# Sending the stacked q/k pieces of an attention kernel in four-head groups, in 64 KB transfers, six under way

## The chip, the cores and the metric

The kernel runs on one core of a Trainium2 chip. The metric is the device time of one execution in microseconds, as the median of repeated runs. The program is launched once; everything from the loads of x and of the weights to the stores of the result is in the time.

## What is computed

The reference takes x of shape 4 x 1024 x 256 (four sequences) and applies two layers. Each layer normalises the rows, and adds an attention over 16 heads of 16 channels and a feed-forward part to x.

```
xn = layernorm(x)
x = x + attention0(xn) + ffn0(xn)     # layer 0: rotary positions, causal mask; ffn0 is a router over 32 slots, top 2
xn = layernorm(x)
x = x + attention1(xn) + ffn1(xn)     # layer 1: scores set to 0 (not to -inf) above the diagonal; ffn1 has sign weights
```

## The kernel before, in words

The work is cut into eight **stages**, k = 0 to 7. A stage is one sequence in one layer; the order is (sequence 0, layer 0), (1, 0), (0, 1), (1, 1), and then the same for sequences 2 and 3. The attention of a stage runs in four **groups** g of four heads.

Scores are wanted with float32 accuracy from bf16 matmuls. So q and k are each split into three bf16 pieces, and the products that matter are put under one another along the contracted dimension: QS and KS are stacks of six terms of 16 rows (96 rows), and three more rows of QS carry the negated row maxima, also in three pieces. The way of one stage:

- TensorE projects q and k in eight chunks c = 0 to 7 (`project`, L1012; VectorE finishes them in `projected`, L787). Chunks 0 to 3 hold the first eight heads (ot = 0), chunks 4 to 7 the other eight.
- ScalarE and GpSimd split each chunk in turn: `first_part` (L626, instruction at L633), `first_rest` (L569, L572), `second_part` (L635, L638), `third_part` (L575, L579). The pieces land in `parts`, which has room for eight heads, so `first_part` of chunk 4 has to wait until the first eight heads have been sent on, and that of chunk 0 of the next stage until the second eight have.
- SyncE sends the pieces into the stacks (`send_stack`, L492, the transfers at L500): twelve transfers of 256 KB for eight heads, all issued one behind the other, without a wait between them. A transfer reads 128 partitions of `parts` and writes 16 rows of a stack. Before the first, SyncE waits for the pieces, and for the scores of the stage before to have read the heads that are written over (L497).
- For each group, TensorE makes the scores once for their row maxima (`max_unit`, L1076, matmuls at L1083 and L1086; VectorE reduces them at L915), VectorE splits the maxima, TensorE turns them (L1092), VectorE copies them to nmT (L938), and ScalarE's queue sends nmT, 24 KB, into the three rows of QS (`send_maxima`, L654, the transfer at L658).
- Then TensorE makes the transposed scores with the maxima already taken off (`scores`, L1094, L1108 and L1111; the first one of a group waits for that transfer, L1098), ScalarE exponentiates (L673), and TensorE multiplies with the values (`weighted_values`, L1114, L1128).

The work of several stages overlaps: while stage k is in its scores, the projections, pieces and stacks of stage k + 1 are made. All engines take their steps **in an order that a planner on the host writes out beforehand** (`plan`, L83, and `run_plan`, L264). The planner gives each step a cost, a due time, a list of steps that it comes after, and a lag until others see its result; at each point it takes, for each engine, the step that can start first, and among equals the one due first. On the chip the order is fixed: a step that waits holds up all that stands behind it on its engine. The planner books a stack of eight heads with 27 us on SyncE and a lag of 3 us (L147), sent when the pieces are there and the stage before has finished the second of the two groups (L146); `first_part` of chunk 4 comes after it (L137). It books 3.5 us for the transfer of nmT (L205).

SyncE's order also holds the loads of x and the stores of the result (`load_x`, L486, `store`, L503). The load of x for stages 4 and 5 waits for the stores of stages 2 and 3.

Of the kernel before, what the change touches and what calls it, by code (L numbers as in the profile page):

```python
# [15 lines left out]
KC = D // P  # L16
# [14 lines left out]
BANK = 512  # L31
NW = 2 * 2 * KC
W_BANKS, ST_BANKS, PT_SLOTS = 3, 3, 2

# [46 lines left out]
def plan():  # L83
# [4 lines left out]
    def job(eng, step, cost, due, after, lag=60.0):  # L88
        jobs[eng, step] = (cost, due, after, lag)
# [16 lines left out]
    for k, (b, l) in enumerate(STAGES):  # L106
# [27 lines left out]
        for c in range(NW):  # L134
            kind, ot, hf = chunk(c)
            due = at(0.1 + 0.03 * c) if ot == 0 else at(0.5 + 0.05 * (c - 4))
            land = [("sp", ("stack", k, 0))] if ot else ([("sp", ("stack", k - 1, 1))] if k else [])  # L137
            job("pe", ("qk", k, c), mm(1024, 4), due, [("act", ("xT", k, 2 * hf + 1))], PE_LAG)
            job("dve", ("qk", k, c), dv(512) * (4 if l == 0 else 1), due,
                [("pe", ("qk", k, c))] + ([("pool", ("third", k, c - 2))] if c > 1 else [("pool", ("third", k - 1, NW - 2 + c))] if k else []))  # L140
            job("act", ("first", k, c), 640, due, [("dve", ("qk", k, c))] + land)
            job("pool", ("rest", k, c), 1180, due, [("act", ("first", k, c))])
            job("act", ("second", k, c), 640, due, [("pool", ("rest", k, c))])
            job("pool", ("third", k, c), 1180, due, [("act", ("second", k, c))])
        for ot in range(KC):
            gone = [("pe", ("st", k - 1, 2 * ot + 1, NEX - 1))] if k else []  # L146
            job("sp", ("stack", k, ot), 27000, at(0.2) if ot == 0 else at(0.7),  # L147
                [("pool", ("third", k, 4 * ot + 3))] + gone, 3000.0)
        xt = [("act", ("xT", k, i)) for i in range(4)]
        if l == 0:  # L150
            job("pe", ("router", k), 1700, at(0.22), xt, PE_LAG)
# [38 lines left out]
        for g in range(NG):  # L190
            gs = t0 + g * tg
            for i, (seg, qb, j, n, wd, diag) in enumerate(MAXU):
                due = gs - tg + 0.8 * tg * i / NMX
                job("pe", ("max", k, g, i), mm(n * wd, 1) + 60 * n * diag, due, [("sp", ("stack", k, g // 2))], PE_LAG)
                before = ("rows", k, g - 1) if g else (("rows", k - 1, NG - 1) if k else None)
                job("dve", ("max", k, g, i), dv(n * wd), due, [("pe", ("max", k, g, i))]
                    + ([("dve", ("split",) + before[1:])] if before else []))
            last = [("dve", ("max", k, g, i)) for i in range(NMX)]
            job("dve", ("split", k, g), 1100 + 400 * l, gs - 0.2 * tg, last + ([("dve", before)] if before else [])
                + ([("pool", ("ev", past[-1], g))] if l and past else []))  # L200
            job("pe", ("rows", k, g), 60, -1.0, [("dve", ("split", k, g))], PE_LAG)
            sent = [("act", ("send",) + before[1:])] if before else []
            job("dve", ("rows", k, g), 230, -1.0, [("pe", ("rows", k, g))] + sent)
            gone = [("pe", ("st", k - 1, g, NEX - 1))] if k else []
            job("act", ("send", k, g), 100, -1.0, [("dve", ("rows", k, g))] + gone, 3500.0)  # L205
            if l == 1:
                job("act", ("e", k, g), 200, gs - 0.1 * tg, [("dve", ("split", k, g))])
                used = [("dve", ("out", k, g - 1, t)) for t in range(2)] if g else (
                    [("dve", ("out", past[-1], NG - 1, t)) for t in range(2)] if past else [])
                job("pool", ("ev", k, g), 1150, gs, [("act", ("e", k, g))] + used  # L210
                    + [("dve", ("later", k, n)) for n in range(NT)])
            m = 2 * (k * NG + g)
            for u, (half, kb, j, n, w) in enumerate(EXPU):
                due = gs + tg * u / NEX
                ordinal = (k * NG + g) * NEX + u
                free = []
                if ordinal >= ST_BANKS:
                    o = ordinal - ST_BANKS
                    free = [("act", ("exp", o // NEX // NG, o // NEX % NG, o % NEX))]
                job("pe", ("st", k, g, u), mm(n * w, 1) + 60 * n * (kb >= 4 * half), due, [("act", ("send", k, g))] + free, PE_LAG)  # L220
                v = PVS.index((half, kb))
                free = []
                if u == PV_FIRST[v]:
                    o = (k * NG + g) * NPV + v - PT_SLOTS
                    free = [("pe", ("pv", o // NPV // NG, o // NPV % NG, o % NPV))] if o >= 0 else []
                job("act", ("exp", k, g, u), ac(n * w), due, [("pe", ("st", k, g, u))] + free)
            for v, (half, kb) in enumerate(PVS):
                due = gs + tg * PV_LAST[v] / NEX - 500
                cols = BANK - max(kb - 4 * half, 0) * P
                free = []  # L230
                if kb == 0 and m + half >= 2:
                    o = m + half - 2
                    free = [("act", ("ocopy", o // 2 // NG, o // 2 % NG, o % 2))]
                job("pe", ("pv", k, g, v), mm(cols, 4) + 60, due, [("act", ("exp", k, g, PV_LAST[v]))] + free
                    + ([("dve", ("v", k, i)) for i in range(4)] if g == 0 and v == 0 else []), PE_LAG)
            for t in range(2):
                due = gs + tg * PV_LAST[HALF_END[t]] / NEX
                o = m + t - 2
                free = [("pe", ("out", o // 2 // NG, o // 2 % NG, o % 2))] if o >= 0 else []
                job("act", ("ocopy", k, g, t), ac(512), due - 600, [("pe", ("pv", k, g, HALF_END[t]))] + free)  # L240
                job("pe", ("out", k, g, t), 460, due, [("act", ("ocopy", k, g, t))], PE_LAG)
                gone = [("pe", ("aT", k - 1, 2 * t + i)) for i in range(2)] if k and g == 0 else []
                job("dve", ("out", k, g, t), 1250 + 1000 * l, due, [("pe", ("out", k, g, t))] + gone
                    + ([("pool", ("ev", k, g))] if l else []))
# [98 lines left out]
def build(nc, a, out):  # L343
    ctx = ExitStack()
    with ctx:
# [86 lines left out]
        normed = Signal(sem("normed"), NT)  # L432
        biased = Signal(sem("biased"))
        part1, rest1, part2, part3 = (Signal(sem(n), NW) for n in ("part1", "rest1", "part2", "part3"))
        stacked = [Signal(sem(f"stacked{o}"), 12, step=16) for o in range(KC)]
        moe_logits = Signal(sem("moe_logits"))
        moe_exp = Signal(sem("moe_exp"))
        suffix_ok = Signal(sem("suffix_ok"), 6)
# [39 lines left out]
        def _(sp):  # L478
# [10 lines left out]
                    sp.wait_ge(*y_out[k % 2].upto(stores_before(k), 0))  # L489
                sp.dma_start(x[:, k % 2, :, :], a["x"][b:b + 1].rearrange("o (n p) d -> p (o n) d", p=P)).then_inc(x_in[k % 2].sem, 16)  # L490

            def send_stack(k, ot):  # L492
                sp.wait_ge(*part3.upto(k, NW // 2 * (ot + 1)))
                sp.wait_ge(*part2.upto(k, NW // 2 * (ot + 1)))
                sp.wait_ge(*part1.upto(k, NW // 2 * (ot + 1)))
                if k:
                    sp.wait_ge(*st_full.upto(k - 1, (2 * ot + 2) * NEX))  # L497
                for term in range(len(Q_PARTS)):
                    for stack, kind, which in ((QS, 0, Q_PARTS), (KS, 1, K_PARTS)):
                        sp.dma_start(stack[term * DH:(term + 1) * DH, ot * HC * T:(ot + 1) * HC * T],  # L500
                                     parts[:, which[term], kind, :]).then_inc(stacked[ot].sem, 16)

            def store(k, h):  # L503
                sp.wait_ge(*empty(("wo", k, 2 * h + 1)))
# [106 lines left out]
        def _(act):  # L611
# [14 lines left out]
            def first_part(k, c):  # L626
                kind, ot, hf = chunk(c)
                act.wait_ge(*empty(("qk", k, c)))
                if c == 4:
                    act.wait_ge(*stacked[0].upto(k, 12))  # L630
                if c == 0 and k:
                    act.wait_ge(*stacked[1].upto(k - 1, 12))
                act.activation(parts[:, 0, kind, hf * BANK:(hf + 1) * BANK], proj[:, c % 2, :], ACT.Copy).then_inc(part1.sem, 1)  # L633

            def second_part(k, c):  # L635
# [338 lines left out]
        def _(pe):  # L974
# [101 lines left out]
            def max_unit(k, g, i):  # L1076
                seg, qb, j, n, wd, diag = MAXU[i]
                bank = bank_for(("max", k, g, i))
                if i == 0:
                    pe.wait_ge(*stacked[g // 2].upto(k, 12))  # L1080
                for q in range(n):
                    h = (g * GH + j + q) * T
                    mm = pe.matmul(bank[:, q * wd:(q + 1) * wd], QS[0:KR, h + qb * P:h + (qb + 1) * P],  # L1083
# [78 lines left out]
def tables():  # L1162
    half = DH // 2
    inv = (np.float32(1.0) / np.power(np.float32(10000.0), np.arange(half, dtype=np.float32) / np.float32(half))).astype(np.float32)
    freqs = np.arange(T, dtype=np.float32)[None, :] * inv[:, None]
    cos = np.repeat(np.cos(freqs), HC, axis=0).astype(np.float32)
    sin = np.repeat(np.sin(freqs), HC, axis=0).astype(np.float32)
    return np.concatenate([cos, cos]), np.concatenate([sin, -sin])


# [37 lines left out]
```

## Time and profile before

| | us |
|---|---|
| median of 3 runs | 1730.38 |
| lowest, highest | 1730.19, 1731.06 |
| the profiled execution, its own time | 1736.93 |
| its span, from the first to the last instruction | 1735.2 |
| TensorE matmul busy (share of the span) | 1551.3 (89%) |
| VectorE busy | 1204.3 (69%) |
| ScalarE busy | 803.8 (46%) |
| GpSimd busy | 238.6 (14%) |
| mean granted TensorE clock, as a share of 2.4 GHz | 0.947 |

The terms below are held against the profiled execution, which was 6.55 us longer than the median. Busy shares are averages over stages that differ; what stops TensorE in a stretch is read from the waits and from the chain of work that ended last.

### The profile page before, as it was taken

To read this page: it belongs to the slowest core of one execution; us is meant where nothing else is said; L and a number is where in the kernel's file an instruction comes from. 1 tells how busy PE (TensorE), PEld (TensorE's weight loads), DVE (VectorE), ACT (ScalarE), POOL (GpSimd) and SP (SyncE) were. 2 spreads that over 40 slices of the span, in tenths; PEclk is the share of its full clock that TensorE was granted. 3 is DMA by queue.
4 is the path that set the end of the run, shared out by engine and by line. 5 is a ranking of instruction groups with operands and counts; after the bars stand their busy time and mean duration, and the time that the engine had idled before them with its cause. 6 is when DMAs were issued, how large, how long until landed. Compare 5 with 4: busy or idle time off the path is not lost.

```text
span 1735.2 us, 26902 instructions
## 1 busy us (share of the span) xinstructions
PE 1551.3 (89%) x10398; PEld 807.8 (47%) x10398; DVE 1204.3 (69%) x2674; ACT 803.8 (46%) x1548; POOL 238.6 (14%) x196
## 2 busy tenths in 40 slices
PE   2787995999999999997959989899999998999998
PEld 1444443464445544463424644445444564446444
DVE  7864873767776777778747678676677677776871
ACT  1112443446555555634434456244555554553655
POOL 5221201102021211112011002010211121021000
PEclk9888897999999989998989999899999999999998
DMA  4336033042063206070230341502406150607000
GB/s 165 39 35 74 2 37 38 1 52 24 10 66 45 31 2 74 11 113 1 33 42 1 45 79 15 60 1 30 45 2 74 19 57 2 74 2 98 2 2 25
DMA packets 44095, 66.28 MB, mean 38 GB/s; under 512 B 7328, under 2 KB 18880, under 8 KB 43968
## 3 DMA queue, kind: packets, MB, share of 16 engines
q1 hardware_dynamic: 40800, 63.77, 28.9%
q8 instruction: 83, 1.36, 0.4%
q10 hardware_dynamic: 3168, 0.79, 0.3%
q14 instruction: 44, 0.36, 0.1%
HBM read 9.23 MB, written 4.19 MB: 8 GB/s over the span
## 4 chain that ended last, share of the span: by engine, by line
PE 75%; DVE 13%; DMA 6%; ACT 3%; issue 2%; SPq 1%; POOL 0%; DVEq 0%; ACTq 0%; POOLq 0%
PE WB L984 22%; PE O L1128 16%; PE WB L1083 14%; PE ST L1108 14%; DMA QS<-nmT 5%; PE ST L1111 3%; PE WB L1086 3%; DVE mxa L915 3%; ACT PT L673 2%; DVE rope_b L805 2%; PE WB L1136 1%; DVE mxb L915 1%; PE WB L1009 1%; PE WB L1050 1%; DVE WB L808 1%
## 5 line engine op out<-in xcount | busy, mean ns | idle before, releaser
L673 ACT ACTIVATE PT<-ST 128x512 f32<-128x512 f32 (+1 forms) x1216 | 626.1, 577 | 595.3 <-PE ST L1111 460.1
L915 DVE TENSOR_REDUCE mxa<-WB 128x1 f32<-128x512 f32 (+3 forms) x864 | 537.5, 664 | 161.6 <-PE WB L1086 94.5
L1108 PE MATMUL ST<-QS,KS 99*128 99x512 bf16 (+3 forms) x1536 | 436.3, 337 | 68.0 <-DMA QS<-nmT 53.4
L1083 PE MATMUL WB<-KS,QS 96*128 96x512 bf16 (+3 forms) x1536 | 454.8, 339 | 17.3 <-DVE proj L809 5.6
L1128 PE MATMUL O<-PT,Vaug 128*17 128x512 f32 (+3 forms) x3072 | 323.6, 497 | 5.6 <-ACT PT L673 3.3
L1108 PEld LDWEIGHTS ST<-QS,KS 99*128 99x128 bf16 x1536 | 149.6, 100 | 256.3 <-ACT PT L673 102.2
L1083 PEld LDWEIGHTS WB<-KS,QS 96*128 96x128 bf16 x1536 | 148.9, 100 | 251.4 <-DVE mxa L915 77.6
L915 DVE TENSOR_REDUCE mxb<-WB 128x1 f32<-128x384 f32 (+3 forms) x352 | 210.3, 635 | 24.1 <-PE WB L1086 22.4
L1086 PE MATMUL WB<-negmask,identb 128*128 128x128 bf16 x1024 | 204.4, 226 | 0.0
L1111 PE MATMUL ST<-negmaskT,identb 128*128 128x128 bf16 x1024 | 201.3, 225 | 0.0
L572 POOL TENSOR_TENSOR proj<-proj,parts 128x512 f32<-128x512 f32 x64 | 73.9, 1160 | 597.8 <-ACT parts L633 597.6
L1086 PEld LDWEIGHTS WB<-negmask,identb 128*128 128x128 bf16 x1024 | 103.7, 101 | 28.4 <-issue 14.3
L1111 PEld LDWEIGHTS ST<-negmaskT,identb 128*128 128x128 bf16 x1024 | 103.3, 101 | 13.6 <-issue 2.1
L1128 PEld LDWEIGHTS O<-PT,Vaug 128*17 128x17 f32 x3072 | 52.7, 96 | 111.1 <-ACT PT L673 66.9
L567 POOL TENSOR_TENSOR x<-x,brow 128x2048 f32<-128x2048 f32 x8 | 36.3, 4539 | 373.3 <-DVE xn L784 373.3
L633 ACT ACTIVATE parts<-proj 128x512 bf16<-128x512 f32 x64 | 39.5, 629 | 90.2 <-DVE proj L809 52.4
L579 POOL TENSOR_TENSOR parts<-proj,parts 128x512 bf16<-128x512 f32 x64 | 73.8, 1159 | 41.2 <-ACT parts L638 41.2
L984 PE MATMUL WB<-xT,w_k 128*128 128x512 f32 x128 | 65.8, 638 | 9.5 <-DVE attn L956 4.3
L805 DVE SCALAR_TENSOR_TENSOR rope_b<-WB,bcol,sin 64x512 f32<-64x512 f32 x64 | 48.0, 750 | 37.3 <-PE WB L984 36.1
L984 PE MATMUL WB<-xT,w_q 128*128 128x512 f32 x128 | 67.8, 655 | 1.5 <-DVE proj L809 1.2
L984 PE MATMUL WB<-w_u,xT 128*128 128x512 f32 x128 | 64.8, 631 | 2.2 <-DVE Vaug L898 1.9
L651 ACT ACTIVATE ghT<-WB 128x512 f32<-128x512 f32 x32 | 19.1, 597 | 93.3 <-PE WB L1050 92.1
(140 smaller groups left out, 1402.9 us busy)
## 6 DMA issues: line engine op xcount, KB each, us to landing
QS<-parts SPq DMA_DIRECT2D x96, 256.0 KB, 13.7
KS<-parts SPq DMA_DIRECT2D x96, 256.0 KB, 15.2
x<-in_x SPq DMA_DIRECT2D x4, 1024.0 KB, 5.5
out<-x SPq DMA_DIRECT2D x8, 512.0 KB, 13.5
QS<-nmT ACTq DMA_DIRECT2D x32, 24.0 KB
w_q<-in_w_q SPq DMA_DIRECT2D x2, 256.0 KB, 6.2
w_k<-in_w_k SPq DMA_DIRECT2D x2, 256.0 KB, 6.1
cos<-in_cos SPq DMA_DIRECT2D x1, 512.0 KB, 5.4
```

What stands on the lines that cost most here:

```text
L572: pool.tensor_tensor(proj[:, c % 2, :], proj[:, c % 2, :], parts[:, 0, kind, hf * BANK:(hf + 1) * BANK], ALU.subtract).then_inc(rest1.sem, 1)
L579: pool.tensor_tensor(parts[:, 2, kind, tok], proj[:, c % 2, :], parts[:, 1, kind, tok], ALU.subtract).then_inc(part3.sem, 1)
L633: act.activation(parts[:, 0, kind, hf * BANK:(hf + 1) * BANK], proj[:, c % 2, :], ACT.Copy).then_inc(part1.sem, 1)
L673: act.activation(PT[:, q % PT_SLOTS, j:j + n, 0:wd], src, ACT.Exp, scale=float(SCALE[STAGES[k][1]])).then_inc(exp_done.sem, 1)
L805: ins = dve.scalar_tensor_tensor(rope_b[to:to + P // 2, :], bank[half, :], bcol[half, kind, ot:ot + 1], sin[half, tok], ALU.add, ALU.mult)
L915: dve.tensor_reduce(dst, bank, AX.X, ALU.max).then_inc(emptied, 1)
L984: mm = pe.matmul(dst, lhsT, rhs, start=(i == 0), stop=(i == len(pairs) - 1))
L1083: mm = pe.matmul(bank[:, q * wd:(q + 1) * wd], QS[0:KR, h + qb * P:h + (qb + 1) * P], KS[0:KR, h + seg * BANK:h + seg * BANK + wd], start= ...
L1086: mm = pe.matmul(bank[:, (q + 1) * wd - P:(q + 1) * wd], identb[:, :], negmask[:, :], start=False, stop=True)
L1108: mm = pe.matmul(ST[:, o + i * wd:o + (i + 1) * wd], KS[0:KM, h + kb * P:h + (kb + 1) * P], QS[0:KM, h + q0:h + q0 + wd], start=True, stop ...
L1111: mm = pe.matmul(ST[:, o + i * wd:o + i * wd + P], identb[:, :], negmaskT[:, :], start=False, stop=True)
L1128: mm = pe.matmul(O[32 * j:32 * j + VA, (half + 1) * BANK - cols:(half + 1) * BANK], Vaug[:, kb, h * VA:(h + 1) * VA], PT[:, slot, j, 0:col ...
```

## The change

A stack is sent for four heads at a time, in 24 transfers of 64 KB. A transfer reads 32 partitions of `parts` and writes 8 rows of a stack (even or odd channels, `par`). There are six semaphores, the lanes; transfer n takes lane n mod 6 and is issued only when the transfer before it on that lane has landed. Whoever waited for a stack now waits for all six lanes. For this the columns of Wq and Wk (and the rotary tables) are laid out on the host so that the four heads of a group lie on 32 neighbouring partitions. The planner's stack step is now for four heads, with 13.5 us on SyncE and a lag of 2.5 us, after the stage before has finished that one group; the planned cost of a step of `weighted_values` rises from 60 to 230 ns above its columns.

```diff
+LANES = 6
-            land = [("sp", ("stack", k, 0))] if ot else ([("sp", ("stack", k - 1, 1))] if k else [])
+            land = [("sp", ("stack", k, g)) for g in (0, 1)] if ot else ([("sp", ("stack", k - 1, g)) for g in (2, 3)] if k else [])
...
-        for ot in range(KC):
-            gone = [("pe", ("st", k - 1, 2 * ot + 1, NEX - 1))] if k else []
-            job("sp", ("stack", k, ot), 27000, at(0.2) if ot == 0 else at(0.7),
-                [("pool", ("third", k, 4 * ot + 3))] + gone, 3000.0)
+        for g in range(NG):
+            gone = [("pe", ("st", k - 1, g, NEX - 1))] if k else []
+            job("sp", ("stack", k, g), 13500, at(0.2 + 0.1 * g) if g < 2 else at(0.5 + 0.1 * g),
+                [("pool", ("third", k, 4 * (g // 2) + 3))] + gone, 2500.0)
...
-                job("pe", ("max", k, g, i), mm(n * wd, 1) + 60 * n * diag, due, [("sp", ("stack", k, g // 2))], PE_LAG)
+                job("pe", ("max", k, g, i), mm(n * wd, 1) + 60 * n * diag, due, [("sp", ("stack", k, g))], PE_LAG)
...
-                job("pe", ("pv", k, g, v), mm(cols, 4) + 60, due, [("act", ("exp", k, g, PV_LAST[v]))] + free
+                job("pe", ("pv", k, g, v), mm(cols, 4) + 230, due, [("act", ("exp", k, g, PV_LAST[v]))] + free
...
-        stacked = [Signal(sem(f"stacked{o}"), 12, step=16) for o in range(KC)]
+        lane = [Signal(sem(f"stack_lane{i}"), 16, step=16) for i in range(LANES)]
...
-            def send_stack(k, ot):
+            def send_stack(k, g):
+                ot, hh = g // 2, g % 2 * 32
...
                 if k:
-                    sp.wait_ge(*st_full.upto(k - 1, (2 * ot + 2) * NEX))
+                    sp.wait_ge(*st_full.upto(k - 1, (g + 1) * NEX))
+                n = 0
                 for term in range(len(Q_PARTS)):
                     for stack, kind, which in ((QS, 0, Q_PARTS), (KS, 1, K_PARTS)):
-                        sp.dma_start(stack[term * DH:(term + 1) * DH, ot * HC * T:(ot + 1) * HC * T],
-                                     parts[:, which[term], kind, :]).then_inc(stacked[ot].sem, 16)
+                        for par in range(2):
+                            turn = lane[n % LANES]
+                            if k or g or n >= LANES:
+                                sp.wait_ge(*turn.upto(k, 4 * g + n // LANES))
+                            src = parts[par * 64 + hh:par * 64 + hh + 32, which[term], kind, :]
+                            row = term * DH + par * (DH // 2)
+                            sp.dma_start(stack[row:row + DH // 2, g * GH * T:(g + 1) * GH * T], src).then_inc(turn.sem, 16)
+                            n += 1
...
                 if c == 4:
-                    act.wait_ge(*stacked[0].upto(k, 12))
+                    for turn in lane:
+                        act.wait_ge(*turn.upto(k, 8))
                 if c == 0 and k:
-                    act.wait_ge(*stacked[1].upto(k - 1, 12))
+                    for turn in lane:
+                        act.wait_ge(*turn.upto(k, 0))
...
                 if i == 0:
-                    pe.wait_ge(*stacked[g // 2].upto(k, 12))
+                    for turn in lane:
+                        pe.wait_ge(*turn.upto(k, 4 * g + 4))
...
-    cos = np.repeat(np.cos(freqs), HC, axis=0).astype(np.float32)
+    cos = np.tile(np.repeat(np.cos(freqs), GH, axis=0), (2, 1)).astype(np.float32)
...
-    cols = np.arange(D).reshape(KC, HC, DH // 2, 2).transpose(0, 3, 2, 1).ravel()
+    cols = np.arange(D).reshape(KC, 2, GH, DH // 2, 2).transpose(0, 4, 1, 3, 2).ravel()
```

## Rows read from the trace of the kernel before

**Rows 1.** The page's chain of work that ended last: shares by engine, by line

```profile
PE 75%; DVE 13%; DMA 6%; ACT 3%; issue 2%; SPq 1%; POOL 0%; DVEq 0%; ACTq 0%; POOLq 0%
```

**Rows 2.** Waits of TensorE: engine, line, releaser: us in total, times, longest

```profile
PE ST L1108 <- DMA QS<-nmT: 53.4, 8, 18.1
```

**Rows 3.** TensorE's timeline where it stood longest: start, us, instruction, idle before

```profile
159.56 0.61 PE L1108 MATMUL ST<-QS,KS 99*128 99x512 bf16 x1 [9.57 <-DMA QS<-nmT]
...
277.24 0.61 PE L1108 MATMUL ST<-QS,KS 99*128 99x512 bf16 x1 [18.07 <-DMA QS<-nmT]
...
886.15 0.61 PE L1108 MATMUL ST<-QS,KS 99*128 99x512 bf16 x1 [16.32 <-DMA QS<-nmT]
...
1109.47 0.61 PE L1108 MATMUL ST<-QS,KS 99*128 99x512 bf16 x1 [5.49 <-DMA QS<-nmT]
```

**Rows 4.** The chain in order of time: transfers of nmT on it, start, us

```profile
211.15 2.67 DMA QS<-nmT
...
255.16 22.03 DMA QS<-nmT
```

**Rows 5.** Issues of stack transfers, all (L500), and two ends of one stack on SyncE

```profile
L500 SPq DMA_DIRECT2D QS<-parts x96: 547/610/994, 71.7 to 1574.0; - x96
...
246.41 0.55 SPq L500 DMA_DIRECT2D QS<-parts  x1
...
253.53 0.62 SPq L500 DMA_DIRECT2D KS<-parts  x1
```

**Rows 6.** Stretches: busy us (instructions) of PE, PEld, DVE, ACT, POOL; PEclk, DMA share, GB/s

```profile
1.90:14.00 12.10, 0.63 (x2) 0.50 (x2) 5.69 (x2) 1.65 (x3) 11.64 (x8) 1.00 1.01 338
...
74.50:101.00 26.50, 23.12 (x81) 13.94 (x81) 15.16 (x29) 2.99 (x5) 0.00 (x0) 0.88 1.03 108
...
255.00:277.00 22.00, 4.17 (x18) 1.92 (x15) 4.97 (x9) 0.00 (x0) 0.00 (x0) 0.65 0.96 101
277.00:370.00 93.00, 91.39 (x605) 46.31 (x606) 63.83 (x124) 47.56 (x92) 9.17 (x8) 0.97 0.01 1
```

**Rows 7.** DMA queue of ScalarE (packets, MB, share), and the issues on it

```profile
q10 hardware_dynamic: 3168, 0.79, 0.3%
...
QS<-nmT ACTq DMA_DIRECT2D x32, 24.0 KB
```

**Rows 8.** ScalarE's timeline: the first piece of chunk 4, in stages 0, 1, 2 and 7

```profile
101.80 1.15 ACT L633 ACTIVATE parts<-proj 128x512 bf16<-128x512 f32 x2 [2.51 <-DMA KS<-parts]
...
296.12 1.19 ACT L633 ACTIVATE parts<-proj 128x512 bf16<-128x512 f32 x2
...
504.60 1.14 ACT L633 ACTIVATE parts<-proj 128x512 bf16<-128x512 f32 x2
...
1518.82 1.15 ACT L633 ACTIVATE parts<-proj 128x512 bf16<-128x512 f32 x2 [0.52 <-DMA KS<-parts]
```

**Rows 9.** SyncE's timeline: first transfers of the stacks of stage 0 and stage 2

```profile
71.66 0.67 SPq L500 DMA_DIRECT2D QS<-parts  x1
...
72.37 0.59 SPq L500 DMA_DIRECT2D KS<-parts  x1
...
473.97 0.55 SPq L500 DMA_DIRECT2D QS<-parts  x1
```

**Rows 10.** Stage 2's last third piece of chunks 0 to 3, and the next nmT

```profile
434.18 1.15 POOL L579 TENSOR_TENSOR parts<-proj,parts 128x512 bf16<-128x512 f32 x1 [0.74 <-ACT parts L638]
...
436.10 0.76 ACTq L658 DMA_DIRECT2D QS<-nmT  x1
```

**Rows 11.** SyncE around the store of stage 2, and VectorE's first use of the load

```profile
741.11 0.60 SPq L500 DMA_DIRECT2D KS<-parts  x1
749.32 5.33 SPq L506 DMA_DIRECT2D out<-x  x2
767.29 0.38 SPq L490 DMA_DIRECT2D x<-in_x  x1
...
777.93 2.70 DVE L746 BATCH_NORM_STATS2 stats<-x 128x6 f32<-128x256 f32 x8
```

More of the change, by code:

```diff
@@ L1165, in tables @@
     freqs = np.arange(T, dtype=np.float32)[None, :] * inv[:, None]
-    cos = np.repeat(np.cos(freqs), HC, axis=0).astype(np.float32)
-    sin = np.repeat(np.sin(freqs), HC, axis=0).astype(np.float32)
+    cos = np.tile(np.repeat(np.cos(freqs), GH, axis=0), (2, 1)).astype(np.float32)
+    sin = np.tile(np.repeat(np.sin(freqs), GH, axis=0), (2, 1)).astype(np.float32)
     return np.concatenate([cos, cos]), np.concatenate([sin, -sin])
```

## The prediction

> **What bounds the kernel now.** I read the shares of the chain first: 75% of it is TensorE, 6% a DMA [rows 1]. TensorE is the bound, so what counts is what makes it stand idle. Its waits, ordered by what ended them, have one DMA at their head: the first score matmul of a group waited for the transfer of nmT, 53.4 us in 8 waits, the longest 18.1 [rows 2]. Four of them, 9.57, 18.07, 16.32 and 5.49 us, are 49.5 us of that [rows 3]. The reader should see that this is no property of the transfer. On a quiet chip nmT takes 2.67 us from its issue to the first matmul; issued at 255.16, just after a stack whose twelve transfers went out from 246.41 to 254.15, it takes 22.03 us, the time in which that stack drains [rows 4, 5]. In that stretch TensorE is busy 4.17 of 22 us at a granted clock of 0.65, against 0.97 in the stretch behind it [rows 6]; 1.0 is 2.4 GHz, so part of it ran at the 1.2 GHz level after the wait. A small transfer stands behind 3 MB. The change is aimed there: never more than 6 x 64 KB ahead of it.
>
> So much speaks for it. Against it stands a second reading, of the rate. While the inputs load, the 16 DMA engines are full (share 1.01) and move 338 GB/s; while a stack is sent they are just as full (1.03) and move 108 GB/s [rows 6]. The loads write all 128 partitions, the stack 16 rows at a time. The engines are held up by something that depends on the shape, and the change halves the rows again, to 8.
>
> **What a group of 24 transfers takes.** The trace has no transfer to 8 rows, so I bound it. Lower end: SyncE's pace, 24 x 0.61 us [rows 5] + 2.7 us until the last is seen [rows 4] = 17.3 us; the 6 lanes never bind then. Upper end: the rate follows the rows, 54 GB/s, so 1.57 MB take 29.1 us, and with 2 us for the last, 31 us. I take 29 us, near the upper end, because the nearest row is the stack transfer itself: engines full, and rate far below the loads'. The planner books 13.5 + 2.5 = 16 us, so in my case the plan is 13 us short for each group; at the lower end only 1.3.
>
> Of how many engines such a transfer uses, the queue of nmT tells something: 3168 packets in 32 transfers are 99 each, 96 source rows and 3 more, and nmT is written to 3 rows [rows 7]. The Trainium skill (DMA: Bandwidth & Descriptors, "Why a DMA increments its semaphore by 16 and not by 1") says that a transfer runs on the largest number of engines, up to 16, that divides the outermost sizes of both its sides, each adding one to the semaphore: 3 for nmT, which the 3 extra packets agree with, and 8 for the new transfers. The skill (SBUF — State Buffer, "Door 1: The DMA port swizzle") gives 16 neighbouring partitions four ports and about 109 GB/s, which the 108 agrees with, and 8 would reach two; an estimate from that page is 54 GB/s or 29 us a group, a rule against this change, where SyncE's pace alone would give 17.3.
>
> **Part by part**, against the profiled execution (1736.9 us, span 1735.2; the median is 6.5 lower).
>
> 1. Stage 0. The first piece of chunk 4 waits for the first eight heads. They were sent from 71.66 [rows 9] and ScalarE went on at 101.80 after 2.51 us idle [rows 8]. Two groups at 29 us, the second's issue beginning 2 us before the first has landed, end at 71.7 + 56 = 128: 26 us late. Behind that wait on ScalarE stand the copies of the hidden part, and TensorE's banks behind them. VectorE has maxima to reduce meanwhile, so I take 15. Ends: 2 (pace 17.3) and 26.
>
> 2. Stages 1 to 7, same wait. The planner puts ScalarE's step right after the stack's booked landing, now 16 instead of 30 us after the stage before has finished its second group. In the trace the stack of stage 2 is sent at 473.97 and ScalarE's step starts at 504.60, 30 us later; stages 3, 6 and 7 do the same, the last at 1518.82 with a DMA as its releaser [rows 8, 9]. With 29 us the step stands some 13 us too early in a fixed order; the exponentials of the running stage are queued behind it, and TensorE has only three score banks. I take 8 us for each of these four, 32. In stages 1, 4 and 5 ScalarE came to it long after the landing: in stage 1 the stack was issued from 246.41 [rows 5], landed some 30 us later, and the step ran at 296.12 [rows 8], 20 us on. That covers most: 2 each, 6. Sum 38. Ends: 0 and 7 x 13 = 91.
>
> 3. The waits for nmT. At most six transfers ahead: 6 x 29/24 = 7.3 us instead of up to 22. The four long waits shrink to some 4 us of idling each, and the long ones give back their lower clock: -32. But stacks are now sent four times a stage, each starting when a group's scores end, which is about when the next nmT is sent. In stage 1 the pieces of the next stage are ready at 435.33 and nmT leaves at 436.10 [rows 10]; before, nothing was in flight there. I count ten such sends. A wait of 4 us is covered by other matmuls now; with some 7 to 9 us, 3 us each stay: +30. Net -2. Ends: -49 (all four long waits gone, nothing new) and +30.
>
> 4. SyncE itself. It is held by a group for as long as the group takes, where twelve issues took 7.7 us [rows 5]. The last issue before the store of stage 2 was at 741.11, the store left at 749.32, x was loaded at 767.29, and VectorE used it at 777.93 [rows 11]. That stack began 7.1 us before its last issue [rows 5], at 734; with SyncE held for 26 us from there the store moves by some 10 us, and VectorE waits in order for the load. Twice (stages 4 and 5), 4 us each after what VectorE has in hand: +8. Ends: 0 and 20.
>
> 5. Six waits instead of one before a group's maxima on TensorE, 32 x 5 more. The trace has no row for a wait that is already met; between nothing and the 0.04 us that SyncE's program takes from the end of one issue to the next [rows 9], 0 to 6 us: +3. ScalarE's extra waits, twice a stage, are hidden by its idle half (46% busy).
>
> 6. The planner's other order. 170 ns more for each weighted-value step shifts what is put beside what on every engine. Which way, no row tells: 0, with ends of 15 us either way.
>
> Layout and tables are made on the host: nothing on the chip.
>
> Sum: 15 + 38 - 2 + 8 + 3 = +62 us: 1799 for a profiled execution, **1792 us** for the median. This case's own range is 1745 to 1848: down by half of steps 1 and 2 (27) and 20 for the order and the idling; up by 9 in step 1, 32 in step 2 (some 16 us in each of the four stages) and 15 in step 6.
>
> **The rivals.**
>
> A. Transfers flow at SyncE's pace and it is faster. That needs six transfers under way to overlap in the memory where two neighbouring ones didn't before: the new ones alternate between the lower and upper 8 rows of a term, so at any time more than 8 rows are being written. Then a group takes 17.3 us, an nmT has at most 6 x 0.61 = 3.7 us ahead, the long waits give back 45 us, ten new ones cost 1.5 us each, steps 1 and 2 cost 2 + 7, SyncE frees early enough, step 5 costs 3: -18, and some 5 us come back as clock [rows 6]: 1707, with 1685 to 1735 around it. For it: the engines are full without moving much, so they have room. Against it: the twelve transfers of a stack change to other rows after every second one, and drain at 108 GB/s all the same [rows 6]. It decides at about 20 us a group.
>
> B. The rate lies between, a group takes 20 to 22 us, and what the nmT waits give back is paid again at the first pieces (about 7 us of the total for each us of a group): no change, 1730.
>
> C. The worse end of my case, as one mechanism: the wait at chunk 4 is not softened at all, because ScalarE feeds both the score banks and the projections, and every stage pays the full 13 us (91) and stage 0 26: 1730 + 91 + 26 - 2 + 8 + 3 = 1856. It decides where TensorE finds nothing else to do behind a held ScalarE.
>
> That the change doesn't do what it says is no rival here: the queue ahead of nmT is shorter in any case.
>
> **How the numbers follow.** My case has 0.55, C 0.05, A 0.32, B 0.08. Both signs hold much, so the range must reach into A: 1692 to 1848 leaves out the lower part of A (about 0.1) and the tail above. A difference of 0.2% (3.5 us) is about what measurement of this kernel can tell from none. Faster: A's 0.32 with a little of B, 0.33. Same: most of B, 0.07. Slower: 0.60.
>
> **What would show it.** Right: the share of the DMA engines and the rate in a group's stretch (about 54 GB/s, the last landing near 29 us after the first issue); ScalarE idle before the first piece of chunk 4 with a DMA as its releaser, in stage 0 by 15 us or more and in stages 2, 3, 6, 7 by some 8 to 13; no wait for nmT above 10 us, but more of them. Wrong: a group that lands in under 20 us, so that ScalarE's wait stays at 1 to 3 us and TensorE's total on nmT falls below 20; then A holds. If groups are slow and the total is not, ScalarE's wait was covered and step 2 is the mistake.

## The result, and the profile after

The changed kernel takes 1752.78 us (median, 1751.65 to 1756.17), the kernel before 1730.29 us beside it: 22.5 us slower, a ratio of 1.0133 (95% interval 1.0115 to 1.015). The profiled execution took 1751.65 us, with a span of 1749.9.

First the page's chain of work that ended last, shares of the span by engine and then by line. Lines have moved: the stack transfers are L511, the first piece L646, the exponentials L686, the scores L1122, the weighted values L1142.

```profile
PE 70%; DMA 12%; DVE 9%; SPq 3%; ACT 3%; issue 2%; POOL 0%; ACTq 0%; DVEq 0%; POOLq 0%
PE WB L997 20%; PE O L1142 15%; PE ST L1122 13%; PE WB L1097 13%; DMA KS<-parts 5%; DMA QS<-parts 4%; PE ST L1125 3%; SPq L511 3%; DMA QS<-nmT 2%; PE WB L1100 2%; ACT PT L686 2%; DVE mxa L928 2%; DVE rope_b L818 2%; PE WB L1150 1%; PE WB L1022 1%
```

Before, DMAs had 6% of it [rows 1], 5% for nmT, and the stacks were not among the lines that the page lists. Now nmT has 2%, and the stacks themselves (5% and 4%), with SyncE's issues between them (3%), have come in with 12%. The change did what it aimed at, and something else took the place. The waits say what; these are TensorE's (us in total, times, longest):

```profile
PE ST L1122 <- ACT PT L686: 35.2, 26, 9.2
PE ST L1122 <- DMA QS<-nmT: 22.5, 13, 3.6
PE O L1142 <- ACT PT L686: 21.7, 11, 8.3
...
PE WB L997 <- ACT ghT L664: 8.5, 1, 8.5
...
PE WB L1097 <- DMA KS<-parts: 7.6, 1, 7.6
```

The wait for nmT, 53.4 us before [rows 2], is 22.5, and its longest 3.6 instead of 18.1. But TensorE now stands 56.9 us behind ScalarE's exponentials, in pieces of up to 9 us. In the kernel before the same two waits were 15.3 us:

```profile
PE ST L1108 <- ACT PT L673: 12.0, 25, 2.2
...
PE O L1128 <- ACT PT L673: 3.3, 8, 1.0
```

What held ScalarE in the changed kernel stands in its own waits:

```profile
ACT parts L646 <- DMA KS<-parts: 69.9, 8, 14.0
```

Eight waits, one for each stage: the first piece of chunk 4, which may not overwrite `parts` until both groups of the first eight heads have landed. In ScalarE's timeline (start, us, instruction, idle before), stages 0 and 7, to be held against [rows 8], with stage 7's next instruction:

```profile
116.23 1.15 ACT L646 ACTIVATE parts<-proj 128x512 bf16<-128x512 f32 x2 [12.33 <-DMA KS<-parts]
...
1526.86 1.15 ACT L646 ACTIVATE parts<-proj 128x512 bf16<-128x512 f32 x2 [13.97 <-DMA KS<-parts]
1527.91 1.06 ACT L686 ACTIVATE PT<-ST 128x512 f32<-128x512 f32 x2
```

The idle times were 2.51 and 0.52 us. The next instruction behind the held one is an exponential that was long ready, and TensorE comes back with it, after 8.31 us (TensorE's timeline):

```profile
1528.54 0.63 PE L1142 MATMUL O<-PT,Vaug 128*17 128x128 f32 x8 [8.31 <-ACT PT L686]
```

The transfers: SyncE's timeline, the first and the last pair of issues of a quick group (stage 2, g = 0) and of a slow one (stage 7, g = 1), and the first pair of stage 0:

```profile
426.13 1.39 SPq L511 DMA_DIRECT2D QS<-parts  x2
...
442.06 1.39 SPq L511 DMA_DIRECT2D KS<-parts  x2
...
1502.59 1.39 SPq L511 DMA_DIRECT2D QS<-parts  x2
...
1520.71 1.60 SPq L511 DMA_DIRECT2D KS<-parts  x2
...
69.95 1.56 SPq L511 DMA_DIRECT2D QS<-parts  x2
```

In stage 0 two groups, issued from 69.95, let ScalarE go on at 116.23: 46.3 us, or about 23 for each. The slow group of stage 7 went from 1502.59 to ScalarE's start at 1526.86: 24.3 us. The quick one issues a pair every 1.43 us and is never held, which puts it at 17.3 us for the issues and some 2 for the last landing. The planner books 16. The rates in the slow group and then in the quick one (busy us of PE, PEld, DVE, ACT, POOL, then PEclk, DMA share, GB/s):

```profile
1503.00:1526.00 23.00, 17.14 (x123) 8.96 (x123) 12.91 (x29) 5.64 (x12) 1.11 (x1) 0.94 0.50 70
...
426.00:445.00 19.00, 17.84 (x118) 8.56 (x118) 12.57 (x30) 9.31 (x18) 0.10 (x1) 0.82 0.38 85
```

In these two stretches the 16 engines are busy 0.50 and 0.38 of the time, where a stack of before filled them all (1.03) [rows 6].

### The profile page after: what moved, and what is told of

It reads as the page before. It is cut to its first block, busy times and chain, and to the rows that moved or that the text cites. A ratio compares the mean times of both kernels' runs of the same rounds, so it can differ in the third digit from the quotient of the medians.

```text
span 1749.9 us, 27604 instructions
## 1 busy us (share of the span) xinstructions
PE 1558.8 (89%) x10398; PEld 803.3 (46%) x10398; DVE 1191.9 (68%) x2674; ACT 801.0 (46%) x1548; POOL 238.8 (14%) x196
## 4 chain that ended last, share of the span: by engine, by line
PE 70%; DMA 12%; DVE 9%; SPq 3%; ACT 3%; issue 2%; POOL 0%; ACTq 0%; DVEq 0%; POOLq 0%
PE WB L997 20%; PE O L1142 15%; PE ST L1122 13%; PE WB L1097 13%; DMA KS<-parts 5%; DMA QS<-parts 4%; PE ST L1125 3%; SPq L511 3%; DMA QS<-nmT 2%; PE WB L1100 2%; ACT PT L686 2%; DVE mxa L928 2%; DVE rope_b L818 2%; PE WB L1150 1%; PE WB L1022 1%
## 5 line engine op out<-in xcount | busy, mean ns | idle before, releaser
L686 ACT ACTIVATE PT<-ST 128x512 f32<-128x512 f32 (+1 forms) x1216 | 626.7, 578 | 551.9 <-PE ST L1125 397.3
L1122 PE MATMUL ST<-QS,KS 99*128 99x512 bf16 (+3 forms) x1536 | 436.7, 338 | 60.0 <-ACT PT L686 35.2
L1097 PE MATMUL WB<-KS,QS 96*128 96x512 bf16 (+3 forms) x1536 | 457.7, 342 | 25.5 <-DVE proj L822 10.8
L1142 PE MATMUL O<-PT,Vaug 128*17 128x512 f32 (+3 forms) x3072 | 327.6, 501 | 23.9 <-ACT PT L686 21.7
L1122 PEld LDWEIGHTS ST<-QS,KS 99*128 99x128 bf16 x1536 | 149.1, 100 | 254.3 <-ACT PT L686 129.8
L646 ACT ACTIVATE parts<-proj 128x512 bf16<-128x512 f32 x64 | 39.7, 627 | 159.5 <-DMA KS<-parts 69.9
L1142 PEld LDWEIGHTS O<-PT,Vaug 128*17 128x17 f32 x3072 | 51.7, 95 | 132.4 <-ACT PT L686 84.9
L818 DVE SCALAR_TENSOR_TENSOR rope_b<-WB,bcol,sin 64x512 f32<-64x512 f32 x64 | 48.0, 750 | 54.5 <-PE WB L997 53.4
L997 PE MATMUL WB<-w_v,ghT 128*128 128x256 f32 x256 | 65.3, 400 | 8.6 <-ACT ghT L664 8.5
```

What stands on the lines that cost most here:

```text
L686: act.activation(PT[:, q % PT_SLOTS, j:j + n, 0:wd], src, ACT.Exp, scale=float(SCALE[STAGES[k][1]])).then_inc(exp_done.sem, 1)
L818: ins = dve.scalar_tensor_tensor(rope_b[to:to + P // 2, :], bank[half, :], bcol[half, kind, ot:ot + 1], sin[half, tok], ALU.add, ALU.mult)
L997: mm = pe.matmul(dst, lhsT, rhs, start=(i == 0), stop=(i == len(pairs) - 1))
L1122: mm = pe.matmul(ST[:, o + i * wd:o + (i + 1) * wd], KS[0:KM, h + kb * P:h + (kb + 1) * P], QS[0:KM, h + q0:h + q0 + wd], start=True, stop ...
L1142: mm = pe.matmul(O[32 * j:32 * j + VA, (half + 1) * BANK - cols:(half + 1) * BANK], Vaug[:, kb, h * VA:(h + 1) * VA], PT[:, slot, j, 0:col ...
```

## The experiments

The theory: the shorter queue ahead of nmT is a gain; the loss is the planner's, which books a group of four heads with 16 us where it takes 19 to 24, and so puts steps that need a stack too early in orders that can't bend. Rivals: the smaller transfers are too slow whatever the plan says; or the loss comes with the other planner cost (the weighted-value step, 60 to 230 ns).

**e1_truthful_plan.** The changed kernel, one booking altered.

```diff
-            job("sp", ("stack", k, g), 13500, at(0.2 + 0.1 * g) if g < 2 else at(0.5 + 0.1 * g),
-                [("pool", ("third", k, 4 * (g // 2) + 3))] + gone, 2500.0)
+            job("sp", ("stack", k, g), 18500, at(0.2 + 0.1 * g) if g < 2 else at(0.5 + 0.1 * g),
+                [("pool", ("third", k, 4 * (g // 2) + 3))] + gone, 4500.0)
```

> The changed kernel with one planner cost altered: a group's stack is booked with 18.5 us on SyncE and a lag of 4.5 us (23 us in all) in place of 13.5 and 2.5. In the changed kernel's trace a group takes 19 to 23 us to its last packet, and ScalarE stands 69.9 us in 8 waits before the first piece of chunk 4. Theory (the loss is the plan's: steps that need a stack are put 7 us too early in a fixed order): ScalarE's wait falls below 20 us, TensorE's idle time behind ScalarE (56.9 us at the scores and the weighted values) by 30 to 45 us, the time to 1705 to 1725 us, below the kernel before. Rival (the slower transfers themselves cost the time, whatever the plan says): ScalarE's wait stays above 50 us or turns into other waits, the time stays at 1745 to 1760 us.

Measured: 1689.85 us, a ratio to the kernel before of 0.9755 (0.9728 to 0.9781); 63 us less than the changed kernel, with the same transfers. Its waits:

```profile
PE ST L1122 <- DMA QS<-nmT: 17.4, 13, 2.8
PE ST L1122 <- ACT PT L686: 16.0, 25, 2.8
...
ACT parts L646 <- DMA KS<-parts: 10.8, 5, 4.7
```

ScalarE's wait went from 69.9 to 10.8 us, TensorE's behind ScalarE at the scores from 35.2 to 16.0. The rival that the transfers as such cost the time falls: they are the same as in the changed kernel, and the kernel is 42 us faster than the kernel before the change. That gain is not the short queue's alone, as this kernel also keeps the raised cost of the weighted-value step (e3 below). It came out 15 us below the expected 1705 to 1725.

**e9_late_chunk4.** Where in the plan the 63 us lie. The changed kernel with its booking kept, and only ScalarE's step planned at the true time, by an empty step that stands for the landing.

```diff
-            land = [("sp", ("stack", k, g)) for g in (0, 1)] if ot else ([("sp", ("stack", k - 1, g)) for g in (2, 3)] if k else [])
+            land = [("sp", ("landed", k))] if ot else ([("sp", ("stack", k - 1, g)) for g in (2, 3)] if k else [])
...
+        job("sp", ("landed", k), 0, at(0.3), [("sp", ("stack", k, g)) for g in (0, 1)], 7000.0 if k else 12000.0)
...
-            run = {"load": load_x, "stack": send_stack, "store": store}
+            run = {"load": load_x, "stack": send_stack, "store": store, "landed": lambda k: None}
```

> The changed kernel (1752.8 us) with the planner told the truth at one place alone: ScalarE's first piece of chunk 4 is planned 7 us (in stage 0: 12 us) after the booked landing of the second group; SyncE's booking of 13.5 + 2.5 us stays for all else that needs a stack (the first maxima, chunk 0 of the next stage, the stores). Booking the whole truthfully gave 63 us back (1689.9). Theory (nearly all of the loss is ScalarE's wait at chunk 4, with the exponentials behind it): ScalarE's wait for a stack falls from 69.9 to 20 us or less, and 45 us or more come back: 1685 to 1708 us. Rival (the loss is spread over all that needs a stack): 1715 to 1745 us.

Measured: 1701.89 us, ratio 0.9806 (0.9777 to 0.9835). Of the 63 us, 51 come back at this one step; ScalarE's waits:

```profile
ACT parts L647 <- DMA KS<-parts: 8.3, 5, 3.3
```

So most of the loss of the change comes from where the plan puts the first piece of chunk 4. The other 12 us go with what else needs a stack. Two of TensorE's waits hint at where, though no run gives either a price of its own:

```profile
PE ST L1123 <- DMA QS<-nmT: 22.1, 13, 2.9
...
PE WB L1098 <- DMA KS<-parts: 7.9, 1, 7.9
```

The wait for the first stack of stage 0 is as long as in the changed kernel (7.6) and does not appear among the waits of e1; the wait for nmT is 22.1 us, where e1 has 17.4.

**e2_after_pv60 and e3_before_pv230.** The other planner cost, taken back on the changed kernel and put alone on the kernel before.

```diff
-                job("pe", ("pv", k, g, v), mm(cols, 4) + 230, due, [("act", ("exp", k, g, PV_LAST[v]))] + free
+                job("pe", ("pv", k, g, v), mm(cols, 4) + 60, due, [("act", ("exp", k, g, PV_LAST[v]))] + free
```

> The changed kernel with the planned cost of a weighted-value step put back from 230 to 60 ns above its columns; the transfers stay as changed. Theory (the stacks' booking makes the loss, this cost only shuffles the order): within 12 us of the changed kernel's 1753 us, ScalarE's wait for the stack still 40 us or more. Rival (the new order that this cost makes is what loses): 1730 us or less.

Measured: 1759.33 us, ratio to before 1.0146 (1.0119 to 1.0173), 6.5 us above the changed kernel by the medians, with ScalarE's wait at 51.4 us. The two intervals of the ratio overlap (the changed kernel's is 1.0115 to 1.015), so the 6.5 us are not clear of noise. The rival falls: without this cost the change is no better.

```diff
-                job("pe", ("pv", k, g, v), mm(cols, 4) + 60, due, [("act", ("exp", k, g, PV_LAST[v]))] + free
+                job("pe", ("pv", k, g, v), mm(cols, 4) + 230, due, [("act", ("exp", k, g, PV_LAST[v]))] + free
```

> The kernel before with only that planned cost raised from 60 to 230 ns; transfers and stacks as before. Theory (it only shuffles the order): within 12 us of 1730 us, the long waits for nmT still there (40 us or more of TensorE's idle time). Rival (this cost is the loss of the change): 1745 us or more.

Measured: 1714.82 us, ratio 0.9894 (0.9873 to 0.9914). The long waits for nmT are still there (49.3 us in 9 waits), and it is 17 us faster all the same. So my own expectation (within 12 us) was off as well: on the kernel before, this cost alone is a gain. On the changed kernel no gain is shown.

**e4_before_two_lanes.** The gain without the small transfers: the kernel before, its 256 KB transfers to 16 rows, and two of them under way.

```diff
+LANES = 2
-        stacked = [Signal(sem(f"stacked{o}"), 12, step=16) for o in range(KC)]
+        lane = [Signal(sem(f"stack_lane{i}"), 24 // LANES, step=16) for i in range(LANES)]
...
+                n = 0
...
+                        turn = lane[n % LANES]
+                        if k or ot or n >= LANES:
+                            sp.wait_ge(*turn.upto(k, 12 // LANES * ot + n // LANES))
                         sp.dma_start(stack[term * DH:(term + 1) * DH, ot * HC * T:(ot + 1) * HC * T],
-                                     parts[:, which[term], kind, :]).then_inc(stacked[ot].sem, 16)
+                                     parts[:, which[term], kind, :]).then_inc(turn.sem, 16)
+                        n += 1
```

(The waits in `first_part` and `max_unit` go over both lanes in the same way.)

> The kernel before, with its twelve transfers of 256 KB to 16 rows, but only two under way: two semaphores, each transfer waits for the one two before it; layout and planner costs as before. This is the change's gain without its smaller transfers. Theory (the gain comes from the short queue ahead of nmT, the loss from the slow groups): a stack still drains in about 30 us, nmT finds at most two transfers (4.6 us) ahead, TensorE's idle time on it falls from 53 to 15 us or less, ScalarE's wait for a stack stays below 15 us, the time is 1690 to 1710 us. Rival (a shorter queue is worth nothing, what TensorE doesn't wait for here it waits for elsewhere): 1725 us or more.

Measured: 1683.68 us, ratio 0.9711 (0.9681 to 0.9741): 48 us gained, with the planner untouched, and somewhat more than the 1690 to 1710 us allowed. TensorE's wait for nmT, and the stretch in which the kernel before stood for 18.07 us [rows 3], stage 0's third nmT:

```profile
PE ST L1117 <- DMA QS<-nmT: 5.4, 6, 2.3
```

```profile
246.00:277.00 31.00, 29.70 (x188) 15.19 (x187) 21.93 (x46) 13.94 (x27) 4.50 (x4) 1.00 0.46 79
```

From 53.4 to 5.4 us, and 48 us of time: nearly all of what TensorE stood behind nmT was time lost. ScalarE's wait for a stack is 9.0 us: the stacks still take what the plan books. In the stretch the granted clock is 1.00; in the wait of before it was 0.65 [rows 6].

**e8_three_lanes.** The same with `LANES = 3`.

```diff
-LANES = 2
+LANES = 3
```

> The kernel before with three transfers of 256 KB under way in place of two (1683.7 us). Theory (each transfer ahead costs nmT 2.3 us, two already fill the engines): stacks still 30 us, TensorE's idle time on nmT up from 5 us to 8 to 15, the time 1683 to 1696 us. Rival (two under way left the engines idle at times, and the stack lands sooner with three): the time below 1680 us.

Measured: 1700.27 us, ratio 0.9809 (0.979 to 0.9829); TensorE's wait for nmT is 17.7 us in 8 waits, the longest 4.5. One transfer of 256 KB more ahead of nmT cost 17 us of the time, somewhat over the 13 that the theory allowed; 12 of them stand in TensorE's wait for nmT. The rival falls.

**e5_two_lanes_short_booking.** The fault by itself: e4 with the stack's booking 7 us too short, on transfers that suit the plan otherwise.

```diff
-            job("sp", ("stack", k, ot), 27000, at(0.2) if ot == 0 else at(0.7),
+            job("sp", ("stack", k, ot), 20000, at(0.2) if ot == 0 else at(0.7),
```

> The kernel before with two transfers of 256 KB under way (1683.7 us), and now with the stack's planned cost on SyncE put from 27 to 20 us: the transfers are the same and still take 30 us, but the plan believes 23. This is the change's fault by itself, 7 us of misbooking, on transfers that are not slow for their plan otherwise. Theory (a booking 7 us short costs what the changed kernel lost against its truthful plan, 63 us, scaled by half as many stacks): ScalarE's wait for a stack rises from 9 to 40 us or more, the time to 1710 to 1750 us. Rival (the planner's order is only shuffled by it): within 10 us of 1684 us.

Measured: 1746.71 us, ratio to before 1.0078 (1.0048 to 1.0107), and 63 us above e4. The waits are those of the changed kernel over again:

```profile
PE ST L1117 <- ACT PT L681: 36.3, 28, 8.3
PE O L1137 <- ACT PT L681: 24.6, 11, 8.3
...
PE ST L1117 <- DMA QS<-nmT: 7.7, 7, 2.1
```

with ScalarE's wait for the stack at 58.9 us in 7. A number in a host-side plan, 7 us wrong, costs 63 us on transfers that did not change. The time lies in the range of the theory, but its scaling did not hold: half as many stacks cost as much. That the two losses are the same 63 us is not explained.

**e6_twelve_lanes.** What sets a group's 19 to 24 us: e1 with twelve lanes.

```diff
-LANES = 6
+LANES = 12
```

(with two transfers a group on each lane instead of four in the counts of the waits)

> The changed kernel with the truthful plan (1689.9 us), now with twelve lanes in place of six. It asks what sets the 19 to 23 us of a group. If six lanes bind (a transfer lands too late for the next on its lane): SyncE no longer waits for lanes, every group takes 18.5 to 19.5 us, and nmT finds up to twelve transfers ahead, so TensorE's idle time on it rises from 17 to 20 to 35 us; time within 10 us of 1690 us. If writing 8 rows at a time is the limit (about 71 GB/s where lanes bound): the slow groups still take 22 to 23 us, issues only come earlier, nmT waits longer all the same, time 1690 to 1710 us.

Measured: 1697.09 us, ratio 0.9789 (0.9764 to 0.9814). SyncE no longer waits for lanes (2.1 us in 9 waits, 39.8 in 142 with six). A group's issues now take 17.1 us; a slow group and a quick one in the same columns as above:

```profile
671.30:694.00 22.70, 22.45 (x186) 9.97 (x185) 19.08 (x46) 14.93 (x30) 1.11 (x1) 1.00 0.50 71
406.90:425.40 18.50, 17.61 (x110) 7.36 (x111) 11.11 (x24) 8.57 (x17) 0.00 (x0) 0.72 0.38 87
```

The slow group was issued by 688.4 and its DMA share stays at 0.50 and 71 GB/s to the end of the stretch. So it isn't the six lanes that make a group slow: with twelve a slow one drains no faster. In others the same transfers keep up with SyncE. TensorE's wait for nmT was 18.7 us, hardly more than with six lanes; the first reading expected 20 to 35, and the second a longer wait too, so neither had this right.

**e7_two_lanes_pv230.** The two gains together: e4 with the weighted-value cost of e3.

```diff
-                job("pe", ("pv", k, g, v), mm(cols, 4) + 60, due, [("act", ("exp", k, g, PV_LAST[v]))] + free
+                job("pe", ("pv", k, g, v), mm(cols, 4) + 230, due, [("act", ("exp", k, g, PV_LAST[v]))] + free
```

> The kernel before with two transfers under way, and the planned cost of a weighted-value step raised from 60 to 230 ns, as the change has it. On the kernel before this cost alone gave 17 us, on the changed kernel 6.5. Theory (it gives TensorE's order a truer price, and adds to the shorter queue): 1660 to 1678 us. Rival (both take away the same idle time, or it only shuffles): 1680 us or more.

Measured: 1671.41 us, ratio 0.9643 (0.9622 to 0.9664). They nearly add (48 and 17 alone): 61 us below the kernel before beside it, 81 below the changed kernel. With two transfers under way the planner cost gains 12 us. It is the fastest version of the study, without smaller transfers and without a new layout.

## Why the prediction was right or wrong

It was right that the kernel gets slower, and why: the mechanism, with ScalarE held before chunk 4 and TensorE behind it, is the one that the trace and e9 show. It was wrong in size, +62 against +22.5 us. Of its own signs, some came: no wait for nmT above 10 us but more of them (13, the longest 3.6), and ScalarE held in stages 2, 3, 6 and 7, for 6.34, 11.76, 9.24 and 13.97 us (some 8 to 13 forecast). Others did not: no group moved at 54 GB/s or took 29 us, and ScalarE's wait in stage 0 was 12.33 us and not 15 or more. Rival A's sign ("TensorE's total on nmT falls below 20") did not come, though narrowly, with 22.5. Rival B had the length of a group about right (20 to 22 us) and the balance wrong: it forecast no change. By the steps:

- *The length of a group*, taken as 29 us. Measured 19 to 24. Neither end was right. The lower end of 17.3 us had 14.6 for the issues; a quick group's issues alone took 17.3. And the rate did not follow the rows down to 54 GB/s, as the slow group moved 70. By the rule of the Trainium skill that the prediction cites (DMA: Bandwidth & Descriptors, "Why a DMA increments its semaphore by 16 and not by 1"), 8 of 16 engines were to be in use, and the slow group's share of 0.50 agrees with it. The estimate of 54 GB/s that the prediction worked out from two ports of the Trainium skill (SBUF — State Buffer, "Door 1: The DMA port swizzle") is not what was measured, and the measurement decides. Why some groups drain at 85 to 87 GB/s with a share of 0.38 and others at 70 with 0.50 was not tried.
- *Step 1*, +15. TensorE stood 7.6 us for the first stack and 8.5 behind ScalarE: 16.1. The first of the two I had not seen. (The forecast's range counts 9 us above the 15, where the step's own end of 26 leaves 11.)
- *Step 2*, +38. TensorE's idle time behind ScalarE at the scores and weighted values rose from 15.3 to 56.9 us: 41.6. That the term fits is in part luck, as errors offset one another. The plan was short by some 7 us for a group and not by 13. But less of that was softened: in stages 2, 3, 6 and 7 TensorE stood 6.3, 6.1, 9.2 and 8.3 us behind ScalarE's 6.3, 11.8, 9.2 and 14.0, where I let it stand 8 of 13. And stages 1, 4 and 5 were not covered: ScalarE was idle there for 5.4, 5.6 and 5.2 us, and TensorE behind it for 3.5, 4.0 and 4.2, where I allowed 2. By e1, being true to the transfers is worth 63 us in all, where steps 1 and 2 have 53.
- *Step 3*, -2. **This is the step that failed**, the term that was mis-sized. I let the four long waits keep 4 us each and gave ten new ones 3 us, so that about 51 of the 53 us stayed. (By its own figures the four fall from 49.5 to 16 us, -33.5 and not -32, before any clock is given back.) They fell to 22.5, a gain of 31. The long ones kept 1.5 to 2.1 us each, 7 in all; the other nine waits have 15 together, where the kernel before had 4 in four, so the new idling is 11 us and not 30. The size came from the group's length: 6 x 29/24 = 7.3 us ahead of nmT, and "some 7 to 9 us" for a transfer. In the changed kernel's chain of work that ended last, the longest nmT is this one (start, us):

```profile
825.68 5.53 DMA QS<-nmT
```

  Stage 0, g = 2, is the case of the 18.07 us [rows 3]. TensorE's timeline there, and the stretch up to it in the columns of [rows 6]:

```profile
262.62 0.39 PE L1122 MATMUL ST<-QS,KS 99*128 99x512 bf16 x1 [1.96 <-DMA QS<-nmT]
```

```profile
255.00:262.50 7.50, 5.56 (x26) 2.91 (x24) 6.02 (x16) 0.00 (x0) 0.00 (x0) 1.00 0.56 74
```

  TensorE's granted clock is 1.00 there, against 0.65 in the wait of before. And e4 shows the worth of such a wait, 48 us of time for 48 us of wait.
- *Step 4*, +8. The load of x moved the other way; what that is worth in time was not measured. SyncE's timeline after stage 2's last group:

```profile
750.40 1.39 SPq L511 DMA_DIRECT2D KS<-parts  x2
751.83 1.52 SPq L517 DMA_DIRECT2D out<-x  x2
756.55 0.38 SPq L492 DMA_DIRECT2D x<-in_x  x1
```

  The store left 2.5 us later than before, but x was loaded at 756.55 instead of 767.29 [rows 11]: the load waits for the store, so the store landed in under 5 us. In the kernel before the load left 18 us after the store's first issue, about when the stack ahead of it had drained (some 30 us from 734). That the store was late there because of that stack is argued from these times. What I had seen of nmT I should have seen of the store.
- *Step 5*, +3, was not measured alone. e6 doubles those waits and is 7 us slower than e1, with other changes beside it.
- *Step 6*, 0 with ends of 15. By e3 the cost alone gains 17 us on the kernel before, outside the ends. On the changed kernel it is 6.5 by the medians of e2, not clear of noise. "No row tells" was true of the amount. A reason for the sign is at hand, that a step's price that is too low lets the plan promise what TensorE can't keep; no run shows that it is the reason.

With the measured terms the sum is 16 + 42 - 31 - 6.5 = +20, near the 22.5 of the medians (14.7 between the two profiled executions). It is a sum of waits: only those for nmT were priced by a run (e4), the last term is not clear of noise, and steps 4 and 5 stand in it at nothing. Seen from the other end: a short queue, the raised planner cost and a plan that knows the transfers give -42 (e1), and the misbooking +63.

## What to carry to other kernels

In a kernel whose order is written out beforehand, a change of a transfer is two changes: the transfer, and what the plan believes of it. Time the new one from a trace before judging it; 7 us too little in the plan turned a gain of 42 us into a loss of 22. And look at what is queued ahead of a small, urgent transfer. Here it was enough to keep two large ones under way: with the same cost for the weighted values, and transfers booked at their true time in both, that kernel (e7, 1671 us) is 18 us faster than the one with small transfers (e1, 1690).

## What was not expected of the hardware

- A transfer on ScalarE's queue can land as late as what SyncE has issued before it: 22.03 us behind a stack of twelve [rows 4]. With at most two 256 KB transfers ahead TensorE's longest wait for it is 2.3 us, with three 4.5.
- A 64 KB transfer to 8 rows takes SyncE 0.67 us to issue (median in the changed kernel), more than the 0.61 of a 256 KB one to 16 rows [rows 5] (duration in ns, least/median/most):

```profile
L511 SPq DMA_DIRECT2D QS<-parts x384: 659/671/1553, 69.9 to 1603.5; - x192
```

- With 24 of them in a row, twelve allowed under way (e6), they drain at 71 GB/s with an engine share of 0.50 in one group and at 87 GB/s with 0.38 in another. It is much the same with six (70 with 0.50, 85 with 0.38). What decides between the two is open.
